# A tuned attention-and-batchnorm kernel: the order of work written out call by call, Wo on the full array, groups of four images, other PSUM banks, pair-major memory

## The reference

```
q, k, v = Wq x, Wk x, Wv x          # per image [128, 256], 8 heads of d = 16 channels
k = softmax(k, over the 16 channels of a head)
context[h] = k[h] v[h]^T            # 16 x 16, summed over the 256 points
out[h] = context[h]^T q[h]
y = Wo out + x
mean, var of y per channel over all images and points
return (y - mean) * rsqrt(var + 1e-5) * gamma + beta
```

## Time and profile before

| what | value |
|---|---|
| median of 3 runs | 50.72 us (50.45 to 51.0) |
| the profiled execution's own time | 51.0 us |
| its span, first to last instruction | 49.3 us |
| TensorE busy | 37.8 us, 77% |
| VectorE busy | 34.4 us, 70% |
| ScalarE busy | 27.1 us, 55% |
| GpSimd busy | 18.5 us, 37% |
| HBM read, written | 2.36 MB, 2.10 MB |

### The profile page before, as it was taken

How to read it: one execution, slowest core, us unless ns; L and a number is a source line. 1 busy time by engine, 2 the same in 40 slices (tenths; PEclk the granted TensorE clock), 3 DMA queues, 4 the chain that set the end, 5 groups by cost and what they waited for, 6 DMA issues and landing times.

```text
span 49.3 us, 1107 instructions
## 1 busy us (share of the span) xinstructions
PE 37.8 (77%) x377; PEld 32.8 (67%) x377; DVE 34.4 (70%) x90; ACT 27.1 (55%) x61; POOL 18.5 (37%) x28
## 2 busy tenths in 40 slices
PE   3999998499999999999999999999999910000000
PEld 3998996398987789798888979797987900000000
DVE  0009399969999969985996799773744897996000
ACT  0915419997398990692397179836436924900000
POOL 5830003999999979762026007090000000000000
PEclk9999999999999999999999999999999999955555
DMA  0398779810000000000000000000000000199992
GB/s 0 100 291 293 224 241 363 345 60 0 0 0 13 0 0 0 0 7 0 13 0 7 0 0 0 0 0 0 0 0 0 13 0 0 66 333 423 389 386 106
DMA packets 2597, 4.52 MB, mean 92 GB/s; under 512 B 416, under 2 KB 1184, under 8 KB 2592
## 3 DMA queue, kind: packets, MB, share of 16 engines
q1 hardware_dynamic: 2448, 4.33, 25.0%
q10 hardware_dynamic: 144, 0.13, 0.8%
HBM read 2.36 MB, written 2.10 MB: 90 GB/s over the span
## 4 chain that ended last, share of the span: by engine, by line
PE 60%; DVE 11%; DMA 10%; POOL 3%; SPq 2%; ACT 2%; issue 1%; DVEq 1%; POOLq 0%; ACTq 0%
PE banks L432 18%; DMA x_sb<-x_dram 10%; PE banks L505 10%; PE banks L457 10%; PE banks L472 10%; PE banks L489 8%; DVE y_sb L413 6%; PE banks L486 3%; DVE stats L386 3%; POOL x_lo L259 3%; SPq L218 2%; ACT x_hi L282 1%; DVEq L64 1%; DVE mean_var L395 1%; ACT std L314 1%
## 5 line engine op out<-in xcount | busy, mean ns | idle before, releaser
L267 POOL TENSOR_TENSOR probs<-probs,k_inv 128x256 f32<-128x256 f32 (+1 forms) x11 | 8.9, 826 | 8.7 <-DVE k_inv L360 8.6
L259 POOL TENSOR_TENSOR x_lo<-x_sb,x_hi 128x512 fp32r<-128x512 f32 (+1 forms) x7 | 7.8, 1130 | 5.3 <-ACT x_hi L282 5.3
L432 PE MATMUL banks<-wkv_hi,x_hi 128*128 128x256 f32 x32 | 7.3, 310 | 0.2 <-ACT x_hi L282 0.2
L282 ACT ACTIVATE x_hi<-x_sb 128x256 fp32r<-128x256 f32 (+1 forms) x11 | 5.4, 514 | 3.3 <-DMA x_sb<-x_dram 3.2
L341 DVE TENSOR_REDUCE k_max<-banks 128x16 f32<-128x256 f32 (+1 forms) x11 | 5.7, 535 | 2.1 <-PE banks L432 2.0
L432 PE MATMUL banks<-wkv_hi,x_lo 128*128 128x256 f32 x32 | 6.6, 290 | 0.7 <-POOL x_lo L259 0.7
L303 ACT ACTIVATE a_hi<-banks 128x256 fp32r<-128x256 f32 (+1 forms) x9 | 3.2, 361 | 6.3 <-PE banks L489 6.3
L432 PE MATMUL banks<-wkv_lo,x_hi 128*128 128x256 f32 x32 | 6.6, 290 | 0.0
L287 ACT ACTIVATE probs<-probs 128x256 f32<-128x256 f32 (+1 forms) x11 | 5.3, 509 | 1.1 <-DVE probs L348 1.1
L432 PEld LDWEIGHTS banks<-wkv_hi,x_hi 128*128 128x128 f32 x32 | 5.1, 197 | 1.2 <-ACT x_hi L282 0.6
L432 PEld LDWEIGHTS banks<-wkv_hi,x_lo 128*128 128x128 f32 x32 | 5.1, 197 | 0.9 <-POOL x_lo L259 0.9
(11 more groups left out here) (42 smaller groups left out, 57.7 us busy)
## 6 DMA issues: line engine op xcount, KB each, us to landing
x_sb<-x_dram SPq DMA_DIRECT2D x5, 256.0 KB, 5.2
out_dram<-y_sb SPq DMA_DIRECT2D x2, 512.0 KB, 3.0
out_dram<-y_sb SPq DMA_DIRECT2D x3, 256.0 KB, 3.1
x_sb<-x_dram SPq DMA_DIRECT2D x1, 512.0 KB, 6.5
x_sb<-x_dram SPq DMA_DIRECT2D x2, 128.0 KB, 2.8
out_dram<-y_sb SPq DMA_DIRECT2D x2, 128.0 KB, 2.0
w_sb<-w_dram ACTq DMA_DIRECT2D x1, 128.0 KB, 2.9
w_sb<-w_dram SPq DMA_DIRECT2D x1, 128.0 KB, 5.1
```

The source lines that it names most:

```text
L259: nc.gpsimd.tensor_tensor(x_lo[:, p, px], x_sb[:, p, px], x_hi[:, p, px].bitcast(F32), ALU.subtract).then_inc(x_lo_ready, hi - lo)
L267: nc.gpsimd.tensor_tensor(heads, heads, inv.to_broadcast([128, (hi - lo) * CH * HEADS, D]), ALU.mult).then_inc(probs_ready, hi - lo)
L282: nc.scalar.activation(x_hi[:, p, px], x_sb[:, p, px], ACT.Copy).then_inc(x_hi_ready, hi - lo)
L432: last = nc.tensor.matmul(kv_ps(p)[:, g, :], xs[:, p, g * 128:(g + 1) * 128], ws[:, :], start=start and g == CH * image, stop=stop, skip_g ...
```

## The change

`run_slots` is gone. Each engine's calls stand one under the other, with the images they take, (lo, hi). What differs in what is done:

- **Grouping of images.** Softmax stages take pairs all through, save `largest_keys`, `shift_keys` and `exponentials` of images 0 and 1. `context`, `mask_context`, `times_wo`, `copy_u`, `times_wq`, `split_a_hi`, `split_a_lo` take images 4 to 7 and 8 to 11 as groups of four. The last two pairs, (12, 14) and (14, 16), go as pairs; before, images 14 and 15 went alone.
- **Passes.** `project` makes the `x_hi` passes of both images first, then the passes with `wkv_lo`, then the `x_lo` passes; before, image by image.
- **Wo on the full array.** `mask_context` writes all 128 columns of `ct_sb` an image (the two halves, zeros between heads), `times_wo` is one 128 x 128 by 128-column matmul an image.
- **Banks.** Keys and values of pairs 0 to 3 go to banks 4 and 5, 6 and 7, 0 and 1, 2 and 3, later pairs to 0 and 1 or 2 and 3 in turn. y of images 8 to 15 stays in PSUM (banks 0, 1, 2, then 3 and 4). No bank of its own stands by for the second context of the end: every `context` writes bank 4.
- **x_lo of images 2 and 3** is made by GpSimd, not VectorE.
- **DMAs.** The wk/wv weights are loaded by SyncE's queue, ahead of x, no longer by ScalarE's. x and the output lie pair-major in memory, [pair, channel, 512], so that a pair is one block of 256 KB. Images 12 to 15 are loaded as two DMAs, and the outputs are stored by eight DMAs of 256 KB in another order.

The core of the diff (lines of the moved calls are in the orders below):

```diff
-EXTRA = 2
-IN_PSUM = PAIRS - 3
+GROUP = 4
+IN_PSUM = 8
...
 STORES = [
-    (0, 1, [("vector", 0, 1)]),
-    (4, 6, [("vector", 4, 6)]),
-    (1, 2, [("vector", 1, 2)]),
-    (8, 12, [("vector", 8, 10), ("scalar", 10, 12)]),
-    (2, 4, [("vector", 2, 4)]),
-    (12, 16, [("vector", 12, 14), ("vector", 14, 16)]),
-    (6, 8, [("scalar", 6, 8)]),
+    (0, 2, "vector"),
+    (8, 10, "scalar"),
+    (2, 4, "vector"),
+    (4, 6, "vector"),
+    (10, 12, "scalar"),
+    (6, 8, "vector"),
+    (12, 14, "vector"),
+    (14, 16, "scalar"),
 ]
...
-            return 6 if p == EXTRA else 2 * ((p - (p > EXTRA)) % 2)
+            return (4, 6, 0, 2, 0, 2, 0, 2)[image // 2] + image % 2
...
+        def ct_ps(lo, hi):
+            return banks[:, 4, 0:(hi - lo) * T].rearrange("e (b d) -> e b d", d=T)
...
+            sp.dma_start(wkv, w[:, 0:2 * C]).then_inc(wkv_landed, 16)
+            load(0)
...
             def mask_context(lo, hi):
                 dve.wait_ge(ct_ready, hi)
...
+                mask = same_head[:, :].rearrange("e (o t d) -> e o t d", o=1, t=2).to_broadcast([C, hi - lo, 2, T])
+                both = ct_ps(lo, hi).rearrange("e b (o d) -> e b o d", o=1).to_broadcast([C, hi - lo, 2, T])
+                nc.vector.tensor_tensor(ct_sb[:, lo:hi, :].rearrange("e b (t d) -> e b t d", t=2), both, mask,
+                                        ALU.mult).then_inc(ct_masked, hi - lo)
...
+                if lo >= 8:
+                    pe.wait_ge(v_ready, hi - 4)
...
             def context(lo, hi):
+                pe.wait_ge(probs_ready, hi)
+                pe.wait_ge(v_ready, hi)
+                if lo > 0:
+                    pe.wait_ge(ct_masked, lo)
...
                 for image in range(lo, hi):
-                    u = u_ps(p, lo, hi)[:, (image - lo) * C:(image - lo + 1) * C]
-                    for t in range(0, C, T):
-                        last = nc.tensor.matmul(u[t:t + T, :], ct_sb[t:t + T, p, image, :], woT[t:t + T, :],
-                                                start=True, stop=True, tile_position=(t, t), skip_group_check=True)
+                    last = nc.tensor.matmul(u_ps(lo, hi)[:, image - lo, :], ct_sb[:, image, :], woT, start=True,
+                                            stop=True, skip_group_check=True)
...
-        "x_dram": np.ascontiguousarray(x.reshape(B, C, N).transpose(1, 0, 2)),
+        "x_dram": np.ascontiguousarray(x.reshape(PAIRS, 2, C, N).transpose(0, 2, 1, 3)).reshape(PAIRS, C, 2 * N),
```

More of the change, by code:

```diff
@@ L162, in attention_batchnorm, with in_memory, on_chip, outputs @@
         stored = sem("stored")
[L165 to L210, removed]
+        def in_memory(t, lo, hi):
+            if hi - lo == 1:
+                return t[lo // 2, :, lo % 2 * N:(lo % 2 + 1) * N]
+            return t[lo // 2:hi // 2].rearrange("p c n -> c p n")
+        def on_chip(t, lo, hi):
+            if hi - lo == 1:
+                return t[:, lo, :]
+            return t[:, lo:hi, :].rearrange("c (p i) n -> c p (i n)", i=2)
+        def outputs(maker, instruction, done):
+            for lo, hi, engine in STORES:
+                if engine == maker:
+                    source = y_sb[:, lo:hi, :] if lo < IN_PSUM else y_ps(lo, hi)
+                    instruction(y_sb[:, lo:hi, :], source).then_inc(done, 1)
         block = ctx.enter_context(nc.Block())
@@ new lines, in _ @@
+            copy_y(0, 2)
+            split_a_hi(2, 4)
+            exponentials(10, 12)
+            copy_values(10, 12)
+            split_hi(14, 16)
+            copy_y(2, 4)
+            exponentials(12, 14)
+            copy_u(4, 8)
+            copy_values(12, 14)
+            split_a_hi(4, 8)
+            exponentials(14, 16)
+            copy_values(14, 16)
+            copy_y(4, 6)
+            copy_u(8, 12)
+            copy_y(6, 8)
+            split_a_hi(8, 12)
+            copy_u(12, 14)
@@ new lines, in _ @@
+            invert_sums(4, 6)
+            mask_context(2, 4)
+            largest_keys(8, 10)
+            split_a_lo(0, 2)
+            shift_keys(8, 10)
+            sum_heads(6, 8)
+            invert_sums(6, 8)
+            largest_keys(10, 12)
+            shift_keys(10, 12)
+            count_y(0, 2)
+            split_a_lo(2, 4)
+            sum_heads(8, 10)
+            invert_sums(8, 10)
+            largest_keys(12, 14)
+            mask_context(4, 8)
+            shift_keys(12, 14)
@@ new lines, in _ @@
+            sum_heads(10, 12)
+            invert_sums(10, 12)
+            count_y(2, 4)
+            largest_keys(14, 16)
+            shift_keys(14, 16)
+            sum_heads(12, 14)
+            split_a_lo(4, 8)
+            invert_sums(12, 14)
+            mask_context(8, 12)
+            sum_heads(14, 16)
+            invert_sums(14, 16)
+            count_y(4, 6)
+            count_y(6, 8)
+            split_a_lo(8, 12)
+            mask_context(12, 14)
+            mask_context(14, 16)
```

484 lines of the change are left out of this document (281 added, 203 removed).

## The result

| | before | after |
|---|---|---|
| median of 4 runs | 50.86 us (50.45 to 51.6) | 52.62 us (52.49 to 53.59) |
| the profiled execution's own time | 51.0 us | 52.69 us |
| its span | 49.3 us | 51.0 us |
| end of the last statistics in it | 40.26 us | 41.87 us |
| from there to the end of the span | 9.0 us | 9.1 us |

The change makes the kernel **slower: ratio 1.0396** (interval 1.0346 to 1.0446), 1.76 us between the medians. The forecast was 51.9 us. All but 0.1 us of the loss lies ahead of the last statistics.

The account below looks back on a forecast made before the run. TensorE was taken as the bound, with VectorE having half a microsecond in five to spare. Terms -1.85 + 1.1 + 0.7 + 1.26 gave +1.2 us, moving the median from 50.72 to 51.9 us; range 50.1 to 53.0.

Parts of the forecast that it names:

- The likeliest case: Whole kernel: TensorE's shorter list is outweighed by new waits, +1.2 us to 51.9 us, own range 51.3 to 52.5, chance 0.50.
- TensorE's list: TensorE's work behind the first 12.6 us: 1.85 us shorter, from Wo, context neighbours and the last pair.
- the start: Up to the project of images 8 and 9: it starts at 13.73 instead of 12.64, 1.1 us late.
- groups of four: Wo of images 4 to 7 and 8 to 11 waits for longer masks: +0.7 us for two groups, 0.2 to 1.4.
- Wo alone: Wo's matmuls on TensorE: full array 3.78 us in place of tiled 5.74, a gain of 1.95 us.
- the exits: Passes of TensorE behind tiled Wo: slowed by 0.10 us each, three exits counted in Wo's old cost.
- The last two contexts: Both write bank 4, so the context of images 14, 15 waits for the mask of 12, 13: +1.26 us.
- The end: Last statistics steps and output stores: 0 us change, with 0.3 to both sides.
- Layout 0: Pair-major memory for x and output: 0 us, since a row stays 2 KB in both layouts.
- Rival 1: VectorE steps that need their neighbour start as early as any other: +0.3 us, 51.0 us, chance 0.14.
- Rivals 2 and 3: Pair-major blocks load faster, 50.1 us, chance 0.08; TensorE stays the bound nearly throughout, 49.3 us, chance 0.08.
- Rival 4: Wo costs 0.14 us an instruction and VectorE's neighbours all 0.18: +2.2 us, 52.9 us, chance 0.20.

Follow-up runs that it names:

- e2: Kernel before with full-array Wo alone, in the old order, banks and layout: 49.37 us, ratio 0.9697 to the kernel before.
- e1: Changed kernel with Wo in 64 x 64 tiles again and masks of 64 columns an image: 52.60 us, ratio 1.0362 to the kernel before.
- e6: Changed kernel with masks and Wo of each group of four done pair by pair: 52.68 us, ratio 1.0317 to the kernel before.
- e9: Changed kernel with bank 7 for the last context and the mask of 12, 13 ahead of split_a_lo(8, 12): 51.44 us, ratio 1.0159 to before.
- e3: Changed kernel with x and output in the old memory layout [channel, image, point]: 53.00 us, ratio 1.0437 to the kernel before.
- e8: Kernel before with full-array Wo and pair-major x and output in memory: 50.17 us, ratio 0.9648 to the kernel before.
- e7: Changed kernel with four pairs of dependent neighbouring VectorE steps set apart by a step of another pair: 53.69 us, ratio 1.0572 to before.
- e11: Kernel before with full-array Wo alone, run again on a second chip: 49.53 us, ratio 0.9777 to the kernel before.
- e4: Changed kernel with mask_context(12, 14) put ahead of split_a_lo(8, 12) on VectorE: 52.01 us, ratio 1.0242 to the kernel before.
- e10: Changed kernel with key and value banks as before, pair 2 in 6 and 7: 52.95 us, ratio 1.0362 to the kernel before.

## Why the prediction was right in sign and 0.7 us short

The likeliest case came true: TensorE's list got shorter and more than that was spent where results no longer lie ahead of their use. The measured 52.62 us lies just outside that case's own range (51.3 to 52.5) and inside the whole one. Part of the closeness is luck: the start came 0.5 us cheaper than forecast and the groups of four 0.5 us dearer, which cancels, and the term for TensorE's list is right only as a sum.

- **TensorE's list, -1.85: came out at -1.7, as a remainder.** Wo alone was priced at -1.95 us, and both orders say less: 1.1 us in e2, some 1.2 us against e1. The mistake is in the exits. I counted the slow pass behind Wo (0.35 us in place of 0.24) as a cost of tiles that goes with them, but behind full-array Wo it still takes 0.32 (18.29 to 18.61). And ahead of a context full-array Wo takes 0.54 us, so that there only 0.10 is won. Wo by itself is cheaper than taken: 0.36 us a pair ahead of full-array work (17.93 to 18.29) where I had 0.47, 0.91 for four, 0.54 ahead of a context; 3.56 us in all for 3.78. A context of four images takes 1.08 us (21.44 to 22.52), not 2 x 0.61. Against that, Wq of four images costs 0.95 to 1.03 us where two pairs took 2 x 0.43. The half microsecond that Wo didn't give and the list still lost has come from elsewhere in it, and I can't assign it.
- **The start, +1.1: measured +0.58.** The step that failed is the first, "x of images 4 and 5 comes 0.4 later". The loads are issued 0.4 later, but ScalarE takes these images up at 6.97 us, before the 7.36 of the earlier trace rows, and by its row (behind the exponential of image 0) without a wait for the load. The first `sum_heads` starts at 8.00 where I had 8.73. The walk from there held: 5.22 us to the project of 8 and 9, for 5.00. Old layout or new, the four traces with the weights on ScalarE's queue have it at 7.33 to 7.63, the ten with them ahead on SyncE's at 6.55 to 7.84 with a middle of 6.95. That the single queue brings this is a guess; no run moved the weights' load alone. (A slip in the walk, 9.90 + 1.06 = 10.96 and not 10.98, changes nothing.)
- **Groups of four, +0.7: measured +1.16, the term that fell short most.** Place, cause and number of the waits were right. VectorE was not free at the context's end at either group, and for that I gave 0.25 us each. The masks start 0.60 and 0.86 us behind the contexts where 0.2 + 0.25 was taken. e6 shows nearly half of the 1.16.
- **The last two contexts, +1.26: measured 1.41,** and e9 gives 1.32 back. Here the walk from `times_wq` through `split_a_hi`, `split_a_lo` and the mask held step by step.
- **Not in the sum:** 0.15 us for u ahead of a Wq, which the forecast called covered. Against e1 the Wq places cost some 0.5 us in all.
- **The end, 0 ± 0.3: 0.1.** Layout 0: e3 and e8 say so.
- **Rival 1,** neighbours for nothing: the Trainium skill, VectorE: DVE Perf Modes, section "The DRAIN you can't avoid", has it that a semaphore to the next step costs nothing extra. The rows 8.00 to 8.78 and 10.39 to 11.18 beside 9.79 to 10.39 say 0.18 us, and the measurement decides. But e7 shows that this price was not the way to get time back.
- **Rivals 2 and 3** fell with e3 and with the three holes. Rival 4 came near in its time, by another cause: Wo was cheap, the groups were dear.

Sizes aside, what the forecast didn't ask was what each part would be worth by itself. It priced full-array Wo at -1.95 us in the changed schedule. e1 shows that there it is worth nothing and e2 and e11 that in the old one it is worth 1.1 to 1.5. The terms of the sum can't be added apart from each other once TensorE waits for VectorE.

## What to carry to other kernels

Where the tensor engine is full for 5.00 us of five and the engine that feeds it for 4.5, ask of every grouping not what it saves but how late its first result is: masks of four images that Wo must wait for cost 0.5 us (e6), and the two context rows of four saved 0.14 us each (1.08 in place of 2 x 0.61). Put a step whose result is awaited next ahead of one that is merely due (e4: two calls swapped, 0.67 us), and take a saving on the bound engine alone first, in the old order, before a new schedule is written around it (e2 and e11: -1.1 to -1.5 us; in the new order: 0). A wait can be moved by a free bank and still not be won (e10), so look whether the engine behind it has a gap in its list.

## What the runs showed of the hardware

- Four float32 instructions with 128 x 128 weights and 128 columns (a pair's Wo) take 0.36 to 0.37 us at a granted clock of 1.00, 0.09 each; eight on 64 x 64 tiles take 0.58. The full array multiplies zeros too and is quicker.
- The way from the full array to column tiles costs time: the same Wo takes 0.17 us more ahead of a tiled context than ahead of full-array work (0.54 and 0.37 in e2). The Trainium skill, TensorEngine Tiling (Array Packing), section "Key Properties", says that a change of mode drains the engine, without a figure; the traces agree with it.
- The tiled context costs 0.27 us an image in one row of four images (21.44 to 22.52) and 0.31 in a row of two (22.57 to 23.19).
